# Three stack slots in turn, a maximum pass set among the matmuls of the group ahead, and the next block's front moved into attention

## What is computed

```python
x = x + sliding_window_attention(layernorm(x))      # 32 heads of 8, window 128
x = x + ffn(layernorm(x))                           # 256 -> 1024 -> 256, relu, 4-bit weights + LoRA
x = x + delta_layer(layernorm(x))                   # projections, causal conv, l2 norms, delta-rule scan, MLP
x = x + ffn(layernorm(x))                           # the same feed-forward again
...
# attention, for blocks of 128 queries that see the block before and their own block:
scores = jnp.einsum('bhnrd,bhncd->bhnrc', qb, kw) * scale
scores = jnp.where(valid, scores, finfo.min)        # distance 0 to 128, key >= 0
probs = softmax(scores); out = einsum(probs, vw) @ Wo.T
# delta-rule scan, one token after the other:
err = S @ k_t - v_t;  S = S - beta_t * outer(err, k_t);  o_t = S @ q_t
```

## Time and profile before

| | us |
|---|---|
| runs of the program | 1537.77, 1543.97, 1548.41 (median 1543.97) |
| the profiled execution: its own time | 1549.48 |
| its span, first to last instruction | 1547.7 |
| busy in the span: PE, DVE, ACT, POOL | 1138.0, 969.1, 477.7, 172.7 |
| mean granted TensorE clock | 0.819 of full |

### The profile page before, as it was taken

One profiled execution on the slowest core, in us unless ns is written; L12 is line 12 of the kernel. 1 busy time (PEld: TensorE's weight loads), 2 busy tenths in 40 slices (PEclk: granted clock), 3 DMA queues, 4 the chain that ended last, 5 costly groups with the idle time before them and its releaser, 6 DMA issues.

```text
span 1547.7 us, 22181 instructions
## 1 busy us (share of the span) xinstructions
PE 1138.0 (74%) x8568; PEld 752.1 (49%) x8568; DVE 969.1 (63%) x2520; ACT 477.7 (31%) x995; POOL 172.7 (11%) x251
## 2 busy tenths in 40 slices
PE   5378547878877777878877887878887887777037
PEld 3146414555546544665445553655445554565025
DVE  3421376866777576865677575865777576846941
ACT  1024402434323412443332422433333422342011
POOL 2000000400031000400030010400030000400300
PEclk8579757979879887899878887989878887999559
DMA  9430413042211413041211414051301403001000
GB/s 294 40 33 5 55 62 33 2 61 67 31 18 36 50 56 33 2 70 56 35 14 40 54 47 33 1 69 58 40 9 41 64 30 33 1 14 61 0 14 7
DMA packets 112426, 64.76 MB, mean 42 GB/s; under 512 B 49184, under 2 KB 106688, under 8 KB 112320
## 3 DMA queue, kind: packets, MB, share of 16 engines
q1 hardware_dynamic: 109264, 58.19, 22.2%
q10 hardware_dynamic: 3056, 5.15, 1.2%
HBM read 45.73 MB, written 17.17 MB: 41 GB/s over the span
## 4 chain that ended last, share of the span: by engine, by line
PE 45%; DVE 25%; DMA 9%; SPq 7%; ACT 7%; issue 7%; POOL 1%; DVEq 0%; POOLq 0%; ACTq 0%
PE bank L1415 8%; PE bank L1395 5%; PE bank L1400 4%; DMA k_stack<-k_pieces 4%; PE bank L1334 4%; DVE k_l L1112 3%; PE bank L1553 3%; PE bank L1504 3%; DVE lane_buf L327 3%; PE bank L1326 2%; PE bank L1372 2%; PE bank L1576 2%; DVE lane_buf L1082 2%; DMA q_stack<-m_rows 2%; DVE conv L973 2%
## 5 line engine op out<-in xcount | busy, mean ns | idle before, releaser
L649 ACT ACTIVATE probs<-bank 128x512 f32<-128x512 f32 x256 | 149.2, 599 | 164.5 <-PE bank L1400 164.2
L903 DVE TENSOR_REDUCE mx<-bank 128x2 f32<-128x320 f32 x256 | 123.4, 491 | 84.1 <-PE bank L1372 75.2
L1415 PE MATMUL bank<-probs,v_ext 128*16 128x128 f32 x2048 | 160.8, 283 | 15.7 <-ACT probs L649 14.7
L1367 PE MATMUL bank<-edge_mask,identb 128*128 128x64 bf16 x512 | 70.0, 227 | 100.8 <-DMA k_stack<-k_pieces 43.3
L327 POOL TENSOR_TENSOR lane_buf<-state,q_l 128x128 f32<-128x128 f32 x128 | 87.8, 715 | 486.6 <-DVEq L1107 486.6
L1395 PE MATMUL bank<-tri_mask,identb 128*128 128x512 bf16 x256 | 112.8, 441 | 30.2 <-DMA q_stack<-m_rows 30.2
L1082 DVE TENSOR_TENSOR lane_buf<-state,til 128x128 f32<-128x128 f32 x256 | 104.1, 407 | 19.4 <-POOL lane_buf L537 10.1
L1367 PEld LDWEIGHTS bank<-edge_mask,identb 128*128 128x128 bf16 x512 | 35.2, 109 | 160.3 <-DVE mx L903 71.4
L1400 PE MATMUL bank<-q_stack,k_stack 128*128 128x128 bf16 x1024 | 112.4, 239 | 0.0
L1415 PEld LDWEIGHTS bank<-probs,v_ext 128*16 128x16 f32 x2048 | 87.0, 98 | 49.5 <-ACT probs L649 26.1
L1400 PEld LDWEIGHTS bank<-q_stack,k_stack 128*128 128x128 bf16 x1024 | 89.3, 108 | 39.7 <-issue 16.3
(11 more groups left out here) (156 smaller groups left out, 1918.7 us busy)
## 6 DMA issues: line engine op xcount, KB each, us to landing
k_stack<-k_pieces SPq DMA_DIRECT2D x192, 64.0 KB
q_stack<-q_pieces SPq DMA_DIRECT2D x192, 32.0 KB
q_l<-lane_q SPq DMA_DIRECT2D x8, 512.0 KB, 4.0
k_l<-lane_k SPq DMA_DIRECT2D x8, 512.0 KB, 4.7
q_pieces<-conv SPq DMA_DIRECT2D x24, 128.0 KB, 2.1
k_pieces<-conv SPq DMA_DIRECT2D x48, 64.0 KB, 2.0
...
```

Of the source, the lines that this page charges most:

```text
L649: act.activation(probs[:, u % 3], score_bank[u % 3][:], ACT.Exp, scale=float(DK) ** -0.5).then_inc(exp_done, 1)
L903: dve.tensor_reduce(mx[:, g, 2 * v:2 * v + 2], bank[1 + u % 2][:, 0:2 * SPAN].rearrange("p (h k) -> p h k", h=2), AX.X, ALU.max).then_inc( ...
L1367: pe.matmul(edges[:, :, e * W:e * W + SUB], identb[:], edge_mask[:, e * SUB:(e + 1) * SUB].rearrange("p (o s) -> p o s", o=1) .broadcast_t ...
L1415: last = pe.matmul(bank[5][row:row + VE, col:col + W], v_ext[:, b, kb, h, :], probs[:, u % 3, (hp * 2 + kb) * W:(hp * 2 + kb + 1) * W], st ...
```

## The change

**Slots.** The stacks get three slots (`RING = 3`), taken in turn: group g of block n is in slot (4n + g) mod 3. A stack is loaded when the second pass of the group three before it is done (`next_stacks`). Room for it comes from smaller tiles: `VE` 9 for 16, `wbeta` half as wide (its matmuls then write 64 rows for each sequence), `probs` with two buffers for three, masks, `sq` and `x_next` laid over other tiles.

**Order in attention.** The 32 units of the second pass run one after another. `PASS1` puts one first-pass unit in front of most of them: at steps 0 to 7 group 2 of the same block, at steps 12 to 19 group 3, at steps 20 to 27 group 0 of the next block, at steps 28 to 31 the first half of its group 1, whose other four units (`LEFT`) follow at the end. On VectorE the tables give one maximum behind every three scan instructions (`STEP = 3`), so the 32 steps take 24 chunks, and the maxima are split by four instructions for five. Score banks are two for three; the turned maxima go to bank 7 and the values' projection to bank 6.

**Front.** The next block's layer norm is at steps 1 and 3, its queries and keys at steps 8 and 9, the splitting in pieces at steps 9, 10 and 13; `pieces_to_dram` and the loads of three of its stacks stand inside attention in SP's list. `hold` is at step 10. Chunk 27 of the scan comes before `first_residual`, chunk 28 between it and the new `first_apply`, chunks 29 to 31 behind that. The down projections of the last layers write one bank (5) for two. The first block's stacks (three), pads and first pass of two groups stand before the loop.

```diff
 SPAN = W + SUB
-VE = 16
-PER = 4
-MAX_TURN_AT = 5
+VE = DK + 1
+RING = 3
+STEP = 3
+AHEAD = 3
+PASS1 = [(0, s) for s in range(8)] + [(0, s) for s in range(12, 20)] + [(1, s) for s in range(20, 32)]
+LEFT = 4
...
+        def slot(n, g):
+            return (n * NG + g) % RING
+
...
+            def next_stacks(n, g):
+
+                sp.wait_ge(scores2, (n * NG + g - RING + 1) * UPG)
+                load_stacks(n, g)
+                if n == 1 and g < RING:
+                    load_pad(1, slot(n, g))
 
...
             def body(t, scan=True, following=True, front=True):
                 n = t + 1
+                if following:
+                    next_stacks(n, 3)
+                    load_max(n, 2)
                 if front:
-                    load_x(t + 2, scan)
-                if following:
-                    for g in range(2):
-                        load_max(n, g)
-                    for g in range(2, NG):
-
-                        sp.wait_ge(scores2, n * N_UNITS + (g - 1) * UPG)
-                        load_stacks(n, g)
-                    load_max(n, 2)
+                    pieces_to_dram(t + 2)
+                    sp.wait_ge(pieces_out, (t + 2) * 144 + 144)
+                    next_stacks(t + 2, 0)
+                if following:
                     load_max(n, 3)
+                if front:
+                    next_stacks(t + 2, 1)
+                    load_max(t + 2, 0)
+                    next_stacks(t + 2, 2)
+                    load_max(t + 2, 1)
                 if scan:
                     outputs_out(t)
                     outputs_in(t)
                 if front:
-
-                    pieces_to_dram(t + 2)
-                    sp.wait_ge(pieces_out, (t + 2) * 144 + 144)
-                    for g in range(2):
-                        load_stacks(t + 2, g)
-                    if not scan:
-                        load_pad(1)
                     load_residual(t + 2)
                 if following:
                     to_lanes_dma(n, scan)
+                if t + 3 < NB:
+                    load_x(t + 3)
                 if scan:
                     sp.wait_ge(out_ready, t + 1)
...
-        AHEAD = 3
-        MAX_AT = [4 * AHEAD + k // PER for k in range(2 * UPG)] + [61 + k // PER for k in range(2 * UPG)]
-        PIECES_AT = [(g, MAX_AT[(g + 1) * UPG - 1] + 1) for g in range(NG)]
-        OUT_AT, NEXT_AT = (48, 60), (86, 94)
-        CUTS = (25, 29, NC_)
+        MAX_AT = {4 * AHEAD + STEP * s + STEP - 1: (dn, (2 * UPG + at) % N_UNITS) for at, (dn, s) in enumerate(PASS1)}
+        PIECES_AT = {4 * AHEAD + STEP * s + k: (dn, g, k) for dn, g, s in ((0, 2, 8), (0, 3, 20), (1, 0, 28))
+                     for k in range(4)}
+        OUT_AT = {4 * AHEAD + STEP * s + 1: g for g, s in enumerate((11, 19, 27))}
+        FRONT_AT = {4 * AHEAD + STEP * s: what for s, what in ((1, "vars"), (3, "apply"), (9, "queries"), (10, "keys"),
+                                                               (13, "second"))}
+        CUTS = (4 * AHEAD + STEP * N_UNITS) // 4, 28, 29, NC_
```

TensorE's attention and VectorE's body:

```diff
+                if front:
+                    max_pieces(t + 2, 1)
+                if has_scan:
+                    scan(t, CUTS[0], CUTS[1], False, False)
+                if following:
+                    first_residual(n)
                 if has_scan:
                     scan(t, CUTS[1], CUTS[2], False, False)
                 if following:
-                    first_residual(n)
-                if front:
-                    rests_first(t + 2)
+                    first_apply(n)
+                if has_scan:
+                    scan(t, CUTS[2], CUTS[3], False, False)
...
                 if has_scan:
                     half_outputs(t)
-                if front:
-                    rests_second(t + 2)
...
             def scores(n, u):
 
                 g, v = divmod(u, UPG)
+                r = slot(n, g)
+                if u == 0 and n:
+
+                    pe.wait_ge(pairs_copied, n)
                 if v == 0:
-                    pe.wait_ge(m_in[g % 2], (n * (NG // 2) + g // 2 + 1) * 48)
-                if u >= 3:
-                    pe.wait_ge(exp_done, n * N_UNITS + u - 2)
-                pb = score_bank[u % 3]
+                    pe.wait_ge(m_in[r], turns(n, g) * 48)
+                if u >= 2 or n:
+                    pe.wait_ge(exp_done, n * N_UNITS + u - 1)
+                pb = score_bank[u % 2]
...
+                first = {s: (dn, (2 * UPG + at) % N_UNITS) for at, (dn, s) in enumerate(PASS1)}
+                pe.wait_ge(v_done, n + 1)
+                for u in range(N_UNITS + 1):
+                    dn, v = first.get(u, (2, 0))
+                    if dn == 0 or dn == 1 and front:
+                        scores_max(n + dn, v)
+                    if u < N_UNITS:
+                        scores(n, u)
...
+                    if u == N_UNITS and front:
+                        turn_max(n + 1, 0)
+                        scores_max(n + 1, 2 * UPG - LEFT)
+                        scores_max(n + 1, 2 * UPG - LEFT + 1)
...
+                    if u:
                         values(n, u - 1)
...
+                    if u > UPG and u % UPG == 2:
+                        turn_out(n, u // UPG - 1)
+                if front:
+                    for v in range(2 * UPG - LEFT + 2, 2 * UPG):
+                        scores_max(n + 1, v)
+                turn_out(n, NG - 1)
```

349 lines of the change are left out of this document (185 added, 164 removed).

## The result

The changed kernel takes 1645.7 us (median, 1637.99 to 1648.1), where the kernel before took 1541.8 beside it on the same chip. The ratio is 1.066, with a 95% interval of 1.061 to 1.071: slower by 6 to 7%. The profiled execution took 1646.8 us, with a span of 1645.0 and a mean granted clock of 0.832.

What follows compares the result with a forecast made beforehand. It took attention's phases following one another, not one engine, as the bound. Six middle blocks +82, last block -15, first block +37 gave +104 us: 1653 on the profiled 1549.5, forecast as 1647, range 1590 to 1725.

Steps and rivals of the forecast that it cites:

- 1. scores of step 7 done: Start of attention, steps 0 to 7: scores of step 7 at 13.5 us (12 to 16) after attention starts.
- 2. step 12 starts; wait: Group 3's stack in attention: it takes 13.5 us more, step 12 starts at 27.0, TensorE waits 4.
- 3. step 20 starts; wait: Next block's pieces, cast behind step 12's exponential, then its stack: step 20 starts at 53.1 us, TensorE waits 12.
- 4. step 28 starts; wait: Stack for group 1 of the next block, 8.9 then 13.5 us: step 28 starts at 75.5, wait 7 to 8.
- 5. end of attention: Steps 28 to 31 through division and `wo`: 14.6 us, first residual at 90.1 instead of 80.5, 9.6 later.
- 6. half outputs behind the residual: After the first residual: residual, variance, apply and four scan chunks put half outputs 8.4 us behind it, before 4.4.
- A block's growth: Each of six middle blocks: 9.6 us in attention and 4.0 after the first residual, 13.6 together, 82 in all.
- What follows the residual: From first residual to half outputs: scan chunks standing ahead add 4.0 us a block; feed-forward still ends before the sums.
- The first block: Three stacks before the first pass instead of two: second pass starts at 90.2 us, attention lasts 89.6; together +37.
- The rival of hidden loads: Attention: stacks land within their four steps' cover, attention takes 61 us, the time is 1441 us; chance 0.06.
- The one with loads of 7 us: Attention rival: stacks land in 7 us by fixed cost and bytes, attention 69 us, time 1491 us; chance 0.04.
- The balance point: Stack loads: below about 8.7 us each, 4.7 less in each of 22 waited loads, gain and loss balance.

## Why the prediction was right, point by point

The forecast was 1647 us in 1590 to 1725; the runs gave 1645.7. That the two agree to 1 us is luck: in the spans the forecast growth was 6 us too large, and the profiled execution of the kernel before, on which it was built, stood higher above its median than that of the changed one. Its steps, in the block shown, counted from 624.29:

| step of the prediction | forecast | measured |
|---|---|---|
| 1. scores of step 7 done | 13.5 | 12.7 (637.03) |
| 2. step 12 starts; wait | 27.0; 4 | 26.5; 4.64 |
| 3. pieces issued after that | 5.7 | 5.4 |
| 3. pieces to DRAM; stack | 6.9; 13.5 | 8.1; 13.0 |
| 3. step 20 starts; wait | 53.1; 12 | 52.9; 12.1 |
| 4. SP comes to group 1; stack | 8.9; 13.5 | 9.0; 12.6 |
| 4. step 28 starts; wait | 75.5; 7 to 8 | 74.6; 5.3 |
| 5. end of attention | 90.1 | 89.4 |
| 6. half outputs behind the residual | 8.4 | 8.2 |

The sum by parts, all as differences to before: up to the first residual +37 forecast, 34.1 measured (176.9 less 142.8). From there to the second +9.6, measured 8.8. The five blocks after that 13.6 each, measured 12.4 (185.0 less 172.6). Up to the last residual -15.5, measured -15.2. Behind it +4.0, measured 7.5. Together +103 and +97.3, the difference of the spans. The waits for stacks, forecast as some 165 us in all, were 162.3.

- **The waits follow the load** (steps 2 to 4): shown by halving the load. That step 20 waits for the pieces and not for its slot is shown by splitting them one step earlier.
- **A block's growth** was a little too large: attention took 81.0 us before and 89.5 after (means of five blocks), 8.5 more for 9.6. The shown block had 80.5 before.
- **What follows the residual** has the right size: from there to the next attention a block grew by 3.9 us for 4.0, and it is the half outputs, which begin 8.2 us behind the residual for 4.4. But the order that I held to be the cause is not: with the scan ahead of the residual they begin 97.5 us after the attention's start instead of 97.7, and before it was 85.3. So all 12.4 us of a block's growth lie ahead of the half outputs, wherever the chunks stand, and my 9.6 and 4.0 are one delay cut in two by the place of the residual. I had also written that the feed-forward "ends ahead of the sums as before" and passed over what TensorE does in between: it ends 4.8 us ahead of them for 2.0, and the sums run at the lower clock.
- **Behind the last residual** the forecast was 4.0, and 7.5 were measured. There the half outputs began 3.1 us behind the residual before, since no subtractions stand ahead of them in the last block, and 8.2 now: 5.1. From there to the end it is 209.7 us for 207.3, and 205.0 with the scan first; the sums of that block take 2.07 us now, and 1.13 both before and with the scan first.
- **The first block** waits 31.8 us for the pads, with three stacks in front of them, and its second pass starts at 85.0 where I had 90.2; its attention lasts 91.9 us and not the 89.6 I gave. The errors cancel in part, to 2.9 us.
- **The rival of hidden loads**, which ends on the other side, was priced at 1441 us. Its price was wrong: with loads of 4 us this kernel takes 1491. It rested on 61 us of attention. (The one with loads of 7 us was priced at 1491; its own terms add up to 1495, and a load of 7.7 us took 1509.) At steps of 1.53 us the order does run where nothing interrupts it, but the pieces' wait, the wait for the maxima and the lower clock at 1.2 GHz after each left 72.8. With loads cut alike no run shows the new order ahead: 0.975 against 0.967 with half of a load, 0.961 against 0.959 with a sixth. So it could only have won back what the kernel before itself waits for stacks. The balance point, a load of 8.7 us, was about right, but only against the kernel before with its full loads: from 1.066 at 13 us and 0.975 at 7.7 a straight line crosses 1 at 9.2.
- **Page and trace.** By the Trainium skill's "DMA: Bandwidth & Descriptors", section "Anatomy of one DMA", a stack would have landed after 7 us, an estimate. That section's fit is for transfers that GpSimd issues, and these are issued by SyncE; here the traces show 13 us, and 7.7 already for half the bytes. The same page's statement that small descriptors cost more agrees in direction, but runs of 4 and 8 KB gave only 2.4 of the 6 us that lie between.
